# Softmax denominators from first-phase scores and streamed probabilities in the 64-wide attentions of a post-norm decoder kernel

## The reference

```
layer 0: q = LN(x) Wq, (k, v) from LN(x) and LN(ctx) together: 512 + 77 keys, 8 heads of 64;
         the context's keys are rotated (rope)
layer 3: q = x Wq, k, v from ctx: 77 keys, 16 heads of 64
both:    softmax(q k^T / 8) v for each head, heads joined, times Wo (+ bias in layer 3)
```

## Time and profile before

| | |
|---|---|
| median of 3 runs | 3495.7 us (3488.41 to 3497.16) |
| profiled execution | 3504.39 us, span 3502.2 us |
| mean granted TensorE clock | 0.831 |
| TensorE matmul / weight loads busy | 2877.4 us (82%) / 1566.3 us (45%) |
| VectorE, ScalarE, GpSimd busy | 1864.2 (53%), 1025.8 (29%), 519.7 us (15%) |
| chain that ended last | TensorE 64%, VectorE 19%, ScalarE 7% |
| L979 value matmuls | 1792 records, layer 0 and layer 3 |

### The profile page before, as it was taken

How to read it: one execution, slowest core, us unless ns; L and a number is a source line. 1 busy time by engine, 2 the same in 40 slices (tenths; PEclk the granted TensorE clock), 3 DMA queues, 4 the chain that set the end, 5 groups by cost and what they waited for, 6 DMA issues and landing times.

```text
span 3502.2 us, 40399 instructions
## 1 busy us (share of the span) xinstructions
PE 2877.4 (82%) x14574; PEld 1566.3 (45%) x14625; DVE 1864.2 (53%) x4927; ACT 1025.8 (29%) x2060; POOL 519.7 (15%) x801
## 2 busy tenths in 40 slices
PE   6899998779987766898878999988799876678985
PEld 2235566424543443245523356563245434432554
DVE  5443324753565888625354433356446559875253
ACT  2431211254223101551234221113533331025520
POOL 1220000121101442000013100011211125410000
PEclk9998977989987878898679988877899787788975
DMA  4000000100000000000000000000001000000000
GB/s 154 2 1 1 1 1 1 46 2 14 24 24 1 1 24 25 1 2 28 34 7 2 1 0 1 1 23 24 2 19 31 13 1 1 25 25 1 1 4 3
DMA packets 16422, 49.65 MB, mean 14 GB/s; under 512 B 1761, under 2 KB 8801, under 8 KB 14434
## 3 DMA queue, kind: packets, MB, share of 16 engines
q1 hardware_dynamic: 15650, 45.79, 3.8%
q10 hardware_dynamic: 576, 1.29, 0.1%
HBM read 45.43 MB, written 1.05 MB: 13 GB/s over the span
## 4 chain that ended last, share of the span: by engine, by line
PE 64%; DVE 19%; ACT 7%; issue 6%; SPq 1%; POOL 1%; DMA 1%; ACTq 0%; DVEq 0%; POOLq 0%
PE psum L979 8%; PE psum L967 4%; PE psum L564 4%; PE psum L534 3%; DVE keep_s L2216 3%; PE psum L554 3%; PE psum L947 2%; PE psum L1497 2%; PE psum L726 2%; PE psum L1327 2%; PE psum L1789 2%; DVE fs_v_s L2078 2%; DVE mx_s L693 2%; ACT PT_s L630 2%; PE psum L801 2%
## 5 line engine op out<-in xcount | busy, mean ns | idle before, releaser
L630 ACT ACTIVATE PT_s<-psum 128x512 f32<-128x512 f32 (+3 forms) x768 | 340.4, 495 | 250.4 <-PE psum L554 247.2
L690 DVE CUSTOM_DVE_ANT_0 rest_s<-psum,packed_early 128x128 f32<-128x128 f32 (+3 forms) x512 | 226.8, 487 | 166.3 <-PE psum L540 164.2
L396 POOL TENSOR_SCALAR ve<-mv 128x4 f32<-128x4 f32 x48 | 14.4, 301 | 1891.1 <-DVE mv L386 1890.9
L2121 PE MATMUL psum<-packed_early,keep_s 128*128 128x128 f32 x1024 | 176.7, 331 | 132.4 <-DVE keep_s L2216 132.0
L1002 ACT ACTIVATE PT_s<-psum 128x512 f32<-128x512 f32 (+1 forms) x224 | 121.1, 592 | 444.9 <-PE psum L969 444.9
L554 PE MATMUL psum<-QS_s,KS_s 64*128 64x512 bf16 (+3 forms) x768 | 199.5, 354 | 51.8 <-DMA QS_s<-nmT_s 38.5
L540 PE MATMUL psum<-KS_s,QS_s 64*128 64x512 bf16 (+3 forms) x768 | 189.2, 363 | 54.6 <-DVE mx_s L693 29.2
L2078 POOL TENSOR_TENSOR buffer<-sim_s 128x1024 f32<-128x1024 f32 x80 | 188.5, 2368 | 239.3 <-DVE keep_s L2216 237.1
L2121 PEld LDWEIGHTS psum<-packed_early,keep_s 128*128 128x128 f32 x1024 | 146.7, 172 | 168.5 <-DVE keep_s L2216 156.3
L979 PEld LDWEIGHTS psum<-vaug0x_s,PT_s 128*128 128x128 f32 (+1 forms) x1280 | 192.1, 236 | 60.8 <-ACT PT_s L1002 46.9
L979 PE MATMUL psum<-vaug0x_s,PT_s 128*128 128x65 f32 (+1 forms) x1280 | 198.5, 320 | 24.0 <-ACT PT_s L1002 20.2
(11 more groups left out here) (437 smaller groups left out, 5361.6 us busy)
## 6 DMA issues: line engine op xcount, KB each, us to landing
buffer<-packed_experts SPq DMA_DIRECT2D x36, 384.0 KB, 3.3
buffer<-packed_moe SPq DMA_DIRECT2D x4, 2048.0 KB, 8.0
buffer<-packed_cross SPq DMA_DIRECT2D x4, 2048.0 KB, 8.4
buffer<-packed_product SPq DMA_DIRECT2D x4, 1024.0 KB, 4.8
packed_early<-packed_early SPq DMA_DIRECT2D x1, 2654.5 KB
raw_s<-packed_setup SPq DMA_DIRECT2D x1, 1840.0 KB, 7.2
packed_late<-packed_late ACTq DMA_DIRECT2D x4, 314.0 KB, 3.7
QS_s<-nmT_s SPq DMA_DIRECT2D x72, 8.0 KB
```

What stands on the lines that cost most here:

```text
L630: a.activation(PT[:, u // 4 % 2, i, q0_of(c):T], bank[u % 3][:, q0_of(c):T], ACT.Exp, scale=scale).then_inc(exp_done.sem, 1)
L690: v.tensor_tensor_reduce(junk[:, u % 2, 0:w], bank[n % 4][:, 0:w], s.w["causal"][:, T - w:T], 1.0, -3e38, ALU.add, ALU.max, mx[:, j, h:h + ...
L2121: mm = pe.matmul(CT[:, c * P:(c + 1) * P], keep[:, n % KEPT, c * P:(c + 1) * P], s.w["ident"][:], is_transpose=True, start=(h == 0 and c % ...
```

## The change

In both 64-wide cross attentions:

- The queries are stored times -1/8. Copies that exist carry the factor. The ring takes minima of the negated, scaled scores.
- After the minimum ScalarE reads the same bank again (`den`): an exp with the minimum as bias, whose row sum (`accum_out`) is the denominator of that row and key part; the exps themselves go to an unused buffer. The bank is free only after this. Tails have four such exps, one per query block, since the bias differs.
- Scores are issued by pairs of heads, and only the first of a pair waits, for the exps of two pairs back.
- In layer 0 the parts of main and tail are joined (`gap`, `factor`, `total`). Then comes the logarithm (`log`), minus the minimum; this takes the place of the negated maximum in the rows, so the exps of phase two come out divided by their sum.
- The values, without a column of ones, are the weights of the value products, and the probabilities are streamed, 512 columns at once. The two heads lie in the two column halves of the array and of one bank, which alternates from pair to pair. The result is already turned: one VectorE copy (`evac`) puts it into `attT`. Reciprocals, multiplies, transposes and the ScalarE copy fall away.
- The value products of a unit are planned behind the scores of the next. The planned length of a unit goes from 2.6 to 2.1; the step between the phases gets 3.6 more in layer 0 and 1.8 more in layer 3.

```diff
-    D1, D2 = 0.8, 2.6
+    D1, D2 = 0.8, 2.1
     plan = []
     for n in range(len(ring)):
-        plan += [(at + D1 * n, "score", n), (at + D1 * n + 1.0, "max", n)]
-    Tm = at + D1 * len(ring) + 1.0
-    plan += [(Tm, "split", 0), (Tm + 1.5, "turn", 0), (Tm + 2.2, "rows", 0)]
-    T2 = Tm + 3.0
+        plan += [(at + D1 * (n // 2 * 2), "score", n), (at + D1 * n + 1.0, "max", n), (at + D1 * n + 1.8, "den", n)]
+    Tm = at + D1 * len(ring) + 2.0
+    if has_main:
+        plan += [(Tm, "gap", 0), (Tm + 0.6, "factor", 0), (Tm + 1.2, "total", 0)]
+        Tm += 1.8
+    plan += [(Tm, "log", 0), (Tm + 0.8, "split", 0), (Tm + 2.3, "turn", 0), (Tm + 3.0, "rows", 0)]
+    T2 = Tm + 3.8
     for m in range(PAIRS * NC):
         b = T2 + D2 * m
-        plan += [(b, "st", m), (b + 0.9, "exp", m), (b + 2.2, "value", m)]
+        plan += [(b, "st", m), (b + 1.0, "exp", m), (b + D2 + 0.1, "value", m)]
         if m % NC == NC - 1:
-            plan += [(b + 3.0, "att", m // NC), (b + 3.9, "turn_pair", m // NC), (b + 4.4, "copy_pair", m // NC)]
+            plan += [(b + D2 + 1.0, "evac", m // NC)]
...
-                if u >= 4:
-                    pe.wait_ge(*scores_read(u - 3))
+                if u >= 4 and u % 2 == 0:
+                    pe.wait_ge(*scores_read(u - 2))
...
-                if c == 0 and i >= 1:
-                    pe.wait_ge(*pair_copied(i))
+                if c == 0 and i >= 2:
+                    pe.wait_ge(*pair_copied(i - 1))
                 for o in range(2):
-                    for j in range(TJ):
-                        mm = pe.matmul(O[o][:, j, :], PT[0:rows, u % 2, o, j * P:(j + 1) * P], vaug[0:rows, c, 2 * i + o, :],
-                                       start=(c == 0 and j == 0), stop=(c == NC - 1), skip_group_check=True)
+                    mm = pe.matmul(bank[2 + i % 2][half(o), :], values[0:rows, c, 2 * i + o, :], PT[0:rows, u % 2, o, :],
+                                   start=(c == 0), stop=(c == NC - 1), tile_position=(0, 64 * o), skip_group_check=True)
                 mm.then_inc(value_done.sem, 1)
-            elif kind == "turn_pair":
-                pe.wait_ge(*att_ready(2 * u + 2))
-                for j in range(TJ):
-                    mm = pe.transpose(bank[2][:, j * P:(j + 1) * P], pairs[:, u % 2, j].rearrange("p o d -> p (o d)"), s.w["ident"][:])
-                mm.then_inc(pair_turned.sem, 1)
...
+            if kind == "den":
+                form, h, j = ring[u]
+                a.wait_ge(*lows_ready(u + 1))
+                if u >= 4:
+                    a.wait_ge(*scores_read(u - 3))
+                junk = PT[:, u // 2 % 2, u % 2, :]
+                if form == "main":
+                    ins = a.activation(junk, bank[u % 4][:], ACT.Exp, bias=low[:, 1, j, h:h + 1], scale=-1.0, accum_out=den[:, 1, j, h:h + 1])
+                else:
+                    for jj in range(TJ):
+                        ins = a.activation(junk[:, jj * LC:(jj + 1) * LC], tail_scores(u)[:, jj, :], ACT.Exp, bias=low[:, 0, jj, h:h + 1],
+                                           scale=-1.0, accum_out=den[:, 0, jj, h:h + 1])
+                ins.then_inc(scores_read.sem, 1)
+            elif kind == "factor":
+                a.wait_ge(*gap_ready(1))
+                a.activation(gap[:], gap[:], ACT.Exp).then_inc(factor_ready.sem, 1)
+            elif kind == "log":
+                a.wait_ge(*(total_ready(1) if has_main else scores_read(len(ring))))
+                a.activation(log[:], total[:], ACT.Ln).then_inc(log_ready.sem, 1)
...
-                    a.activation(PT[0:rows, u % 2, o, :], bank[o][0:rows, :], ACT.Exp, scale=scale).then_inc(exp_done.sem, 1)
-            elif kind == "copy_pair":
-                a.wait_ge(*pair_turned(u + 1))
-                a.copy(attT[:, u, :], bank[2]).then_inc(pair_copied.sem, 1)
...
                 if form == "main":
-                    v.tensor_reduce(mxm[:, j, h:h + 1], bank[u % 4][:], AX_X, ALU.max).then_inc(scores_read.sem, 1)
+                    v.tensor_reduce(low[:, 1, j, h:h + 1], bank[u % 4][:], AX_X, ALU.min).then_inc(lows_ready.sem, 1)
                 else:
-                    v.tensor_reduce(mxt[:, :, h], tail_scores(u), AX_X, ALU.max).then_inc(scores_read.sem, 1)
+                    v.tensor_reduce(low[:, 0, :, h], tail_scores(u), AX_X, ALU.min).then_inc(lows_ready.sem, 1)
+            elif kind == "gap":
+                v.wait_ge(*lows_ready(len(ring)))
+                link(v.tensor_tensor(lowest[:], low[:, 0], low[:, 1], ALU.min))
+                v.tensor_tensor(gap[:], lowest[:].unsqueeze(1).to_broadcast([P, S, TJ, H]), low[:], ALU.subtract).then_inc(gap_ready.sem, 1)
+            elif kind == "total":
+                v.wait_ge(*scores_read(len(ring)))
+                v.wait_ge(*factor_ready(1))
+                link(v.tensor_tensor(gap[:], gap[:], den[:], ALU.mult))
+                v.tensor_tensor(total[:], gap[:, 0], gap[:, 1], ALU.add).then_inc(total_ready.sem, 1)
             elif kind == "split":
-                v.wait_ge(*scores_read(len(ring)))
-                if has_main:
-                    link(v.tensor_tensor(mxt[:], mxt[:], mxm[:], ALU.max))
-                link(v.tensor_scalar(mxt[:], mxt[:], -1.0, None, ALU.mult))
+                v.wait_ge(*log_ready(1))
+                link(v.tensor_tensor(log[:], log[:], lowest[:], ALU.subtract))
...
-            elif kind == "att":
+                        link(v.tensor_tensor(log[:], log[:], part[:], ALU.subtract))
+                ins.then_inc(rows_split.sem, 1)
+            elif kind == "evac":
                 v.wait_ge(*value_done(NC * (u + 1)))
-                if u >= 1:
-                    v.wait_ge(*att_ready(2 * u))
-                if u >= 2:
-                    v.wait_ge(*pair_turned(u - 1))
-                for o in range(2):
-                    done(v.reciprocal(rd[:, o, :], O[o][:, :, 64]))
-                    v.tensor_tensor(pairs[:, u % 2, :, o, :], O[o][:, :, 0:64],
-                                    rd[:, o, :].unsqueeze(2).to_broadcast([P, TJ, 64]), ALU.mult).then_inc(att_ready.sem, 1)
+                v.tensor_copy(attT[:, u, :], bank[2 + u % 2]).then_inc(pair_copied.sem, 1)
...
-            copy_out(a.copy, u, copied_a.sem)
+            copy_out(a.copy, lambda to, of: a.activation(to, of, ACT.Copy, scale=-SCALE64), u, copied_a.sem)
...
-                copy_out(v.tensor_copy, u, copied_v.sem)
+                copy_out(v.tensor_copy, lambda to, of: v.tensor_scalar(to, of, -SCALE64, None, ALU.mult), u, copied_v.sem)
```

More of the change, by code:

```diff
@@ L889, in l0_attn, with attend64 @@
     return [attention, errors], branch_psum(s), branch_ready(1)
-def attend64(s, H, qT, kT, tail_at, NK, vaug, chunks, scale, wo, at, ready, bo=None):
+SCALE64 = 64 ** -0.5
+def attend64(s, H, qT, kT, tail_at, NK, values, chunks, wo, at, ready, bo=None):
     PAIRS, NC = H // 2, len(chunks)
     has_main = tail_at > 0
+    S = 2 if has_main else 1
     ring = []
@@ L922, in attend64 @@
+    low = s.tile("low", [P, S, TJ, H])
+    den = s.tile("den", [P, S, TJ, H])
+    gap = s.tile("gap", [P, S, TJ, H])
+    lowest = s.tile("lowest", [P, TJ, H]) if has_main else low[:, 0]
+    total = s.tile("total64", [P, TJ, H]) if has_main else den[:, 0]
+    log = s.tile("log", [P, TJ, H])
     part = s.tile("part", [P, TJ, H], BF16)
@@ L992, in scalar @@
             yield t
-            if kind == "rows":
-                a.wait_ge(*max_turned(1))
-                a.copy(nmT[:], bank[3]).then_inc(max_copied.sem, 1)
+            if kind == "den":
[17 more added lines that the diff above has]
+                a.activation(log[:], total[:], ACT.Ln).then_inc(log_ready.sem, 1)
+            elif kind == "rows":
+                a.wait_ge(*rows_turned(1))
+                a.copy(nmT[:], bank[3]).then_inc(rows_copied.sem, 1)
             elif kind == "exp":
@@ L1056, in l0_xattn @@
     kT = s.tile("kT0x", [P, H // 2, NK])
-    vaug = s.tile("vaug0x", [P, 5, H, 65])
+    values = s.tile("values0x", [P, 5, H, 64])
     kept = s.at
@@ L1078, in tail, with copy_out @@
         return b[:, 0:4 * LC].rearrange("p (g n) -> p g n", g=4)
-    def copy_out(copy, u, sem):
+    def copy_out(copy, negate, u, sem):
         form, g = units[u]
@@ L1083, in copy_out @@
         if form == "q":
-            ins = copy(qT[:, g, :], b[:])
+            ins = negate(qT[:, g, :], b[:])
         elif form == "kl":
@@ L1090, in copy_out @@
             n = toks[g][1]
-            ins = copy(vaug[0:n, g, :, 0:64], b[0:n, :].rearrange("p (h d) -> p h d", d=64))
+            ins = copy(values[0:n, g, :, :], b[0:n, :].rearrange("p (h d) -> p h d", d=64))
         ins.then_inc(sem, 1)
@@ L1170, in vector @@
             else:
-                copy_out(v.tensor_copy, u, copied_v.sem)
+                copy_out(v.tensor_copy, lambda to, of: v.tensor_scalar(to, of, -SCALE64, None, ALU.mult), u, copied_v.sem)
     project = Program(end, tensor=tensor, scalar=scalar, vector=vector, gpsimd=gpsimd)
     s.at = kept
```

(4 more changed lines are left out.)

39 lines of the change are left out of this document (14 added, 25 removed).

## The result

The changed kernel takes 3286.8 us (median of four, 3274.8 to 3292.1) against 3496.4 for the kernel before beside it: ratio 0.9398, 95% interval 0.9373 to 0.9422, faster by 210 us. The profiled execution has a span of 3290.0 us and a mean granted clock of 0.840.

What follows compares the result with a forecast made beforehand. The prediction took TensorE as the bound, with the value matmul the chain's largest line at 8%. Its terms summed to -95 us a turn, -190 in all, from the median 3495.7 to 3305 us, range 3215 to 3420.

Steps and rivals of the forecast that it cites:

- Values: Second-phase value products: four 512-column records in two column halves take 1.05 us a unit; -79 us a turn.
- Clock in the second phases: Second-phase scores and max rows: TensorE has no gap left, so its clock rises to 2.4 GHz and stays; -16 us a turn.
- rival 1: Second phases: the clock does not recover, costing 31 us a turn, about 3370 us; chance 0.16.
- Exps: Second-phase exps: values run under them, leaving a gap of about 0.2 us a unit; -12 us a turn.
- Turns, reciprocals, copies: After the value products: transposes, reciprocals, multiplies and a ScalarE copy go, one VectorE copy comes; -12 us a turn.
- Score pairs: Rings: both scores of a pair always run side by side, a gain in layer 0, stream 0; -8 us a turn.
- The step between phases: From last minimum to second phase: last exp, table load, logarithm; 3.2 us in layer 0, 2.2 in layer 3; +11 a turn.
- Sums in the rings: ScalarE's added exps with sums: +5 us in layer 0, +12 and +4 in layer 3's two rings, a turn.
- neighbours' matmuls at the higher clock: Other stream's matmuls beside the second phases: gain of up to 25 us a turn, not counted in the sum.
- Rival 3: Value products: column tiles run in part one after the other, about 3350 us, wholly in series 3425; chance 0.10.
- rival 4: All rings: ScalarE's place in the loop sets their pace; at 2.2 us a pair 3550 us; chance 0.08.
- Rival 5: Feed-forward windows: the other stream takes the chain over, some 50 us a turn lost, 3405 us; chance 0.06.

Runs made afterwards that it cites:

- run 5: Changed kernel with both heads' value products in the lower column half, one after the other, upper half of the result not computed: 3364.1 us.
- run 3: Changed kernel with a unit's value products put ahead of the next unit's scores again: 3348.6 us.
- run 4: Changed kernel with the ring's scores planned and waited for one by one instead of in pairs: 3302.5 us.
- run 1: Changed kernel without the exps with row sums in the ring, denominators set to ones, output not normalised: 3225.9 us.
- run 7: Changed kernel with the layer 3 ring planned at 1.3 instead of 0.8 a score: 3264.8 us.
- run 6: Changed kernel with layer 3 tails taking one minimum and one 308-column exp, the four sums on VectorE: 3272.0 us.

## Why the prediction was right

3305 was forecast in a range of 3215 to 3420; 3286.8 came. Against the kernel before that is 190 us forecast and 210 measured. The terms, per turn, with the changed kernel's chain summed by line as the forecast summed:

- *Values: -79, and it was about -90.* L979 held 273.8 us of the chain in both turns, L986 holds 93.5. A unit takes 1.01, nearly the assumed 1.05, and some of it lies beneath exps and is out of the chain. That two 64-column tiles overlap as L564's strips do is shown by run 5.
- *Clock in the second phases: -16, and it was -16.* L967 and L969 held 201.2 us in both turns, L975 and L977 hold 168.3. The clock rose to full in all eight second phases, in the first within 10 us of its start, and rival 1 falls. The reason given, no gap at half clock, is not shown: the gap is gone there, but in run 3 a phase with a wait in nearly every unit ran at 0.98 and another at 0.58, and the changed kernel's own units of 2.65 us hold a wait of 1.1 us at full clock.
- *Exps: -12, and -8.* 48.3 to 31.9 us of chain in both turns. The unit of 2.65 us was forecast at 2.75. Run 3 shows that the order is needed for it: with the old order the exps hold 59.3 us.
- *Turns, reciprocals, copies: -12.* L985, L1042, L1043 and L1005 held 33.2 us of the chain in both turns; the new copy L1061 holds 1.9. So -16.
- *Score pairs: -8, measured by run 4 at 16 in both turns.*
- *The step between phases: +11, and about +11.* The four steps of the first turn grew by 18.5 us in all (3.3, 3.9, 10.9 and 0.5), of which 7 go when the sums are left out (run 1); the rest is 11. The total was right and its places in part were not: 3.2 us was put on each step of layer 0, near what came, and 2.2 on each of layer 3, where one grew by 10.9, with both loads bare, and the other by 0.5.
- *Sums in the rings: +5, +12, +4, in all 21, and run 1 gives 30.* This is the term that was mis-sized. "16 tails add 14 to 26, so it needs 30 to 42" was sound: 16 x 1.2 = 19 us, and ScalarE's time in the stretch came to 39. But the ring and its step were taken to be as long as ScalarE's work, while they were 47: TensorE stood at scores whose bank was not free, with the neighbour's work behind them (run 7), and the clock fell to half (0.68, and 0.99 without the sums, run 1), so the scores, too, took nearly twice as long. From first score to copy that is +24, where the forecast had +12 and 2 for the step: 13 in the ring (4.8 of idle TensorE, and some 8.5 from 17 us at half clock, an estimate) and 11 in the step, 4 of these 11 from the sums.

The terms with the values measured here are -90 -16 -8 -16 -8 +11 +30 = -97 a turn, -194, where 210 were measured. The other 16 us are not assigned to a line. Part may be neighbours' matmuls at the higher clock, which the forecast left for the low end, but no run separates them. These terms are sums over the chain for some and differences between runs for others, so they need not add up exactly. That the total came within 20 us is in part luck: the values and the turns, reciprocals and copies gave 15 a turn more than forecast, and the exps and the sums together 13 less.

Rival 3 (tiles in part in series) is refuted by the 1.01, rival 4 by the layer 0 ring, which got shorter, 68 to 62 us between first score and copy; only in layer 3 does ScalarE set the pace. Rival 5 has no sign either: in the landmarks no gain is lost again outside the layer 3 rings, and the 46.1 us up to the second turn are, but for 1, the last second phase (40) and the next layer 0 ring with its step (5).

What stays open is what makes the clock fall and rise. In run 6, with ScalarE no longer the bound, the clock of the ring is still 0.67 although TensorE was idle only 0.91 us in it, and in run 3 two phases with the same waits differ. The runs show what half clock costs, and that it goes from the layer 3 ring when the sums go; that waiting alone brings it is not shown.

## What to carry to other kernels

When one operand of a product is no wider than half the array, make it the weights and stream the long side: two such products side by side cost what one does, and the result may come out in the layout that the next step wants. Order the phases so that the waiting engine's own next block of work, not a neighbour's, covers the wait. And before moving a reduction to another engine for many small blocks, count the instructions per bank that it needs there: when one engine of a ring gives banks back more slowly than planned, the others wait with it, and so does a neighbour in the same in-order queue. What that engine still has queued at the ring's end delays the next step as well (5.8 us here).

## What the hardware showed that was not expected

- A row sum on ScalarE is a second instruction, ACTIVATION_READ_ACCUMULATOR, with 204 to 240 ns of its own in the records; exp of 77 columns and read together start every 0.29 to 0.30 us.
- The clock of the layer 3 ring fell from 1.00 to 0.68 with the sums on ScalarE, with 224 matmul records in the window before and after, and is back at 0.99 without the sums (run 1). With fewer ScalarE instructions and hardly a wait it is still 0.67 (run 6).
- In two column halves, fp32 products of 512 columns with 64 weight columns overlap almost fully: 1.01 us for two, 1.86 in series.
